# Multiplying ones in TensorE's gaps through the routing stage of a convolution-attention and expert kernel on one core

## The chip, the cores and the metric

One core of a Trainium2 chip runs the whole program. The metric is the device time of one execution in microseconds; the median of the runs is compared.

## What is computed

The input x is 2 images of 256 channels by 32 by 32, so 2048 tokens of 256 channels, float32. First comes a layer norm over channels, then an attention block with 1x1 convolutions (queries, keys and values of 128 channels, a global vector beside the map), whose output is added to x. Then each token is normalised again and routed: a softmax over 8 experts, of which the best two count.

```python
gate = softmax(xt @ Wg); topv, topi = top_k(gate, 2)
topv = topv / (sum(topv) + 1e-6); scores = zeros(T, 8).at[topi].set(topv)
for e in range(8):
    h = gelu(xt @ W1[e] + b1[e])          # 256 -> 1024
    out = out + (h @ W2[e] + b2[e]) * scores[:, e:e+1]
```

The result is added to the tokens.

## The kernel before

The kernel is written by hand for each engine: every engine has its own program, in program order, and engines wait for each other on semaphores that count upwards. Nothing is scheduled by a planner.

It has three stages. In the first (to about 95 us) rows are normalised and projected and the attention runs in 16 row blocks. In the second, which overlaps the end of the first, the tokens are normalised again and routed. In the third the experts run over tiles of gathered tokens. Every product of float32 values is made of three matmuls of split operands (`product3`, L1244 to L1246, and L1545, L1547, L1549 in the second layer).

**Routing.** TensorE turns the normalised tokens (`turn_tokens`, L1414, eight turns of four transposes), ScalarE copies each turn out of PSUM (`xt_copy`, L702), TensorE multiplies with the gate's weights (`logits`, L1429, eight times four float32 matmuls of 8 columns). VectorE takes each half of the tokens in turn: `route_gates` finds the two best experts (L1002 to L1030), TensorE counts ranks within each expert (`ranks`, L1439 and L1440), `route_ranks` (from L1040) turns ranks into places, and VectorE, ScalarE and GpSimd write one-hot matrices (`hot_q` L1066, `hot_r` L501, L733, L1075). TensorE multiplies them (`inverse`, L1455) to get the inverse of the placing, ScalarE copies it (`slot_t`, L773), TensorE makes the table of slots (L1514), and VectorE makes from it the row numbers (`row_in` L1158, `row_out` L1160). VectorE's `route_gates(1)` waits for all eight logits, its `hots(1)` for the first inverse.

**The first gather.** GpSimd waits for `row_in`, raises `gathers_begun`, and gathers three blocks of 128 rows with indirect DMAs (L521). TensorE meanwhile multiplies a matrix of ones into a PSUM bank that nobody reads (10 matmuls, L1573), waits for the gather, turns the rows (`turn_x`, L1522), and multiplies ones 8 times more (L1577). ScalarE and VectorE split the turned rows (`x_hi` L780, `x_lo` L1175), and with that the first tile can start.

**The experts.** Each expert has a first tile, of three blocks (`If(odd)`, L1582) or of two (`Else`), and then a hardware loop over further tiles of two blocks (L1587). A loop over pairs of experts holds this text twice, for the even and for the odd expert, so that TensorE's code for a pair is: three-block tile, two-block tile, loop body, and the same again. A tile of two blocks issues 96 matmuls for the two layers and six transposes, a tile of three blocks 120 and six; each comes with a weight load, so that they are 204 and 252 instructions, and some 15 to 20 waits and register instructions. In an expert's first tile the weights of the next are split by ScalarE (`w_hi` L803) and VectorE (`w_lo` L1202) between the pieces of work for this one, and SyncE loads the ones after that (`load_expert`, L350 and L352).

A float32 matmul of ones stands in the trace as two weight loads and two matmuls: the ten of L1573 are 20 records of each.

Of the kernel before, what the change touches and what calls it, by code (L numbers as in the profile page):

```python
# [24 lines left out]
P = 128  # L25
# [27 lines left out]
def metaformer_kernel(nc, x_tok_d, q1_d, q2_d, k1_d, k2_d, v_d, o_d, aff_d, og_d, ob_d,  # L53
                      wg_d, w1_d, b1_d, w2_d, b2_d, out_d):
    ctx = ExitStack()
    with ctx:
        def sb(name, shape, dt=F32, stack=ctx):
            return stack.enter_context(nc.sbuf_tensor(name, shape, dt))

        def sem(name):  # L60
            return ctx.enter_context(nc.semaphore(name))
# [6 lines left out]
        ones = sb("ones", [P, P])  # L68
# [151 lines left out]
        banks = ctx.enter_context(nc.psum_tensor("banks", [P, 8, 512], F32))  # L220
# [50 lines left out]
        xt_copied = sem("xt_copied")  # L271
# [38 lines left out]
        gathers_begun = sem("gathers_begun")  # L310
# [97 lines left out]
        def _(pool):  # L408
# [162 lines left out]
            for e in range(E):  # L571
                _, t1, odd, more = expert_bounds(pool, e)

                odd1 = pool.value_load(bounds[0:1, 1, e:e + 1], min_val=0, max_val=E)
                with pool.If(odd):
                    tile(t0, e, t0 * 2 + odd0, WIDE)
                with pool.Else():
                    tile(t0, e, t0 * 2 + odd0, 2)
                with pool.If(more):
                    with pool.Fori(t0 + 1, t1) as t:  # L580
                        tile(t, e, t * 2 + odd1, 2)
                t0 = t1
                odd0 = odd1
# [6 lines left out]
        def _(act):  # L590
# [224 lines left out]
            for e in range(E):  # L815
                _, t1, odd, more = experts[e]
                with act.If(odd):
                    tile(t0, e, WIDE, True)
                with act.Else():
                    tile(t0, e, 2, True)  # L820
                with act.If(more):
                    with act.Fori(t0 + 1, t1) as t:
                        tile(t, e, 2, False)
                t0 = t1
# [3 lines left out]
        def _(dve):  # L828
# [397 lines left out]
            for e in range(E):  # L1226
                _, t1, odd, more = experts[e]
                prior = e - 1 if e else None
                with dve.If(odd):
                    tile(t0, e, WIDE, True, prior)  # L1230
                with dve.Else():
                    tile(t0, e, 2, True, prior)
                with dve.If(more):
                    with dve.Fori(t0 + 1, t1) as t:
                        tile(t, e, 2, False, e)
                t0 = t1
# [4 lines left out]
        def _(pe):  # L1241
# [155 lines left out]
            def turn_tokens(i):  # L1397

                if i in (1, 3):
                    pe.wait_ge(xn2_more, i + 1)  # L1400
                else:
                    pe.wait_ge(xn2_ready, {0: 2, 2: 4}.get(i, 2 * i - 2))

                if i in (0, 2):
                    pe.wait_ge(o_taken, i + 2)
                elif i == 3:
                    pe.wait_ge(pt_split, 2 * NBLK)
                elif i in (4, 6):
                    pe.wait_ge(ctx_split, 3 + i // 6)
                else:  # L1410
                    pe.wait_ge(xt_copied, {1: 1, 5: 3, 7: 4}[i])
                for j in range(2):
                    for k in range(KC):
                        ins = pe.transpose(banks[:, XT_BANK[i], (KC * j + k) * P:(KC * j + k + 1) * P],  # L1414
                                           xn2[:, 2 * i + j, k * P:(k + 1) * P], ident[:, :])
                ins.then_inc(xt_ready, 1)

            def logits(n):

                pe.wait_ge(xt_copied, n + 1)  # L1420
                if n == 0:
                    pe.wait_ge(pt_split, 2 * NBLK)
                elif n == 4:
                    pe.wait_ge(o_taken, 7)
                half = n // (HALF // 2)
                for i in (2 * n, 2 * n + 1):
                    c = i % HALF * E
                    for k in range(KC):
                        ins = pe.matmul(banks[:, LG_BANK[half], c:c + E], xt2[:, i, k, :], w_g[:, k, :], start=k == 0,  # L1429
                                        stop=k == KC - 1)  # L1430
                ins.then_inc(lg_ready, 1)

            def ranks(half):

                pe.wait_ge(sel_ready, half + 1)
                chosen = sel[:, :, :].rearrange("p e i -> p (e i)")
                pe.wait_ge(o_taken, 6 + 2 * half)
                bank = banks[:, RANK_BANK[half], :]
                pe.matmul(bank[:, 0:E * HALF], below[:, :], chosen, start=True, stop=True)  # L1439
                pe.matmul(bank[:, E * HALF:2 * E * HALF], ones[:, :], chosen, start=True, stop=True  # L1440
                          ).then_inc(rank_ready, 1)

            def inverse(half, k):

                pe.wait_ge(xt_copied, 5)
                for i in range(HALF):
                    m = HALF * k + i
                    pe.wait_ge(hot_q_ready, 2 * HALF * half + m + 1)
                    if k == 1:
                        pe.wait_ge(hot_r_more, HALF * half + i + 1)  # L1450
                    elif i < POOL_HOTS:
                        pe.wait_ge(hot_r_ready, POOL_HOTS * half + i + 1)
                    else:
                        pe.wait_ge(hot_r_rest, (HALF - POOL_HOTS) * half + i - POOL_HOTS + 1)
                    ins = pe.matmul(banks[:, INV_BANK, 0:P], hot_q[:, k, i, :], hot_r[:, k, i, :],  # L1455
                                    start=half == 0 and m == 0, stop=half == 1 and m == 2 * HALF - 1)
                if k == 1:
                    ins.then_inc(inv_ready, 1)


            pe.wait_ge(proj_out, len(PROJ) - 2)
            for step in range(NBLK + 1):
                if step == 1:
# [30 lines left out]
            turn_tokens(3)  # L1494
            logits(2)
            logits(3)
            turn_tokens(4)
            turn_tokens(5)
            logits(4)
            ranks(0)  # L1500
            logits(5)
            turn_tokens(6)
            turn_tokens(7)
            logits(6)
            logits(7)
            inverse(0, 0)
            ranks(1)
            inverse(0, 1)
            inverse(1, 0)
            inverse(1, 1)  # L1510

            pe.wait_ge(inv_taken, 1)
            pe.wait_ge(place_ready, 1)
# [4 lines left out]
            def turn_x(n):  # L1518
                pe.wait_ge(x_gathered, (n + 1) * (16 * WIDE))
                for i in range(WIDE):  # L1520
                    for k in range(KC):
                        ins = pe.transpose(banks[:, 6 + k, i * P:(i + 1) * P], xg[:, i, k * P:(k + 1) * P],  # L1522
                                           ident[:, :])
                ins.then_inc(xg_turned, 1)
# [43 lines left out]

            pe.sem_inc(l2_done, HJ)
            pe.wait_ge(slots_ready, 2)  # L1570

            for _ in range(10):
                pe.matmul(banks[:, 0, 0:P], ones[:, :], ones[:, :], start=True, stop=True)  # L1573
            pe.wait_ge(bounds_ready, 2)
            turn_x(0)
            for _ in range(8):
                pe.matmul(banks[:, 0, 0:P], ones[:, :], ones[:, :], start=True, stop=True)  # L1577
            with pe.Fori(0, E // 2) as pair:
                for n in range(2):
                    e = pair * 2 + n  # L1580
# [36 lines left out]
```

## Time and profile before

| | us |
|---|---|
| median of 3 runs | 424.38 (423.72 to 425.94) |
| the profiled execution | 422.75 |
| its span | 421.0 |
| TensorE busy (matmul) | 371.4, 88% |
| VectorE busy | 268.9, 64% |
| ScalarE busy | 247.4, 59% |
| GpSimd busy | 183.4, 44% |
| mean granted clock of TensorE | 0.919 of 2.4 GHz |

The profiled execution took 1.75 us more than its span, and 1.63 us less than the median. A line of the page stands for all instructions of one source line; "idle before" is the time in which the engine stood still just ahead of them, with what ended it. PEclk is the share of 2.4 GHz that was granted, so that 0.50 is 1.2 GHz. "issue" is a wait that no semaphore of the profile explains.

### The profile page before, as it was taken

Reading aid. Unit: us, or ns where it says so; the run is one execution under the profiler, and the core shown is the slowest. Engines: PE = TensorE matmul, PEld = TensorE weight load, DVE = VectorE, ACT = ScalarE, POOL = GpSimd, SP = SyncE. Lnnn points to the kernel's source line nnn. Section 1 sums busy time; section 2 is a strip of 40 time slices with the busy share of each in tenths; the row PEclk is TensorE's granted clock in tenths of the full one; section 3 lists DMA queues with packets and bytes.
Section 4 is the critical chain, followed back from the end, with each engine's and each line's share of the span. In section 5 each row is a group of like instructions: output and inputs, shape, how many; then the busy total and the mean of one; then the engine's idle time right before and its main releaser. Section 6 shows DMA issues by size and latency. Waiting matters only on the chain.

```text
span 421.0 us, 8173 instructions
## 1 busy us (share of the span) xinstructions
PE 371.4 (88%) x2476; PEld 333.1 (79%) x2477; DVE 268.9 (64%) x709; ACT 247.4 (59%) x522; POOL 183.4 (44%) x271
## 2 busy tenths in 40 slices
PE   5989978998897958799969999999999999999950
PEld 4535457886786947799969999998999999999950
DVE  5857387798789898275526643975549753945530
ACT  1476656657424774385538654986558864955520
POOL 5800000003035534306664556676667637666553
PEclk8689999999998555899997999999999999999995
DMA  8800000000002655707332653278432913333342
GB/s 267 266 20 2 0 1 2 0 2 1 1 2 100 243 184 205 248 8 251 64 65 29 182 119 53 39 245 229 93 61 29 264 39 54 49 55 59 54 59 29
DMA packets 22966, 38.63 MB, mean 92 GB/s; under 512 B 2576, under 2 KB 17296, under 8 KB 22800
## 3 DMA queue, kind: packets, MB, share of 16 engines
q0 software_dynamic: 8032, 12.82, 17.8%
q1 hardware_dynamic: 14896, 25.41, 17.5%
q8 instruction: 11, 0.18, 0.2%
q14 instruction: 27, 0.22, 0.2%
HBM read 28.85 MB, written 9.37 MB: 91 GB/s over the span
## 4 chain that ended last, share of the span: by engine, by line
PE 36%; issue 8%; POOL 6%; DMA 3%; ACT 3%; DVE 3%; POOLq 1%; DVEq 0%; ACTq 0%
PE banks L1244 6%; PE banks L1245 6%; PE banks L1246 6%; PE banks L1545 5%; PE banks L1547 5%; PE banks L1549 5%; POOL xg L521 4%; DMA xg<-xn_rows,idx_in 3%; PE banks L1522 2%; POOL out_rows L567 2%; ACT h_hi L793 1%; DVE y_out L1184 1%; PE banks L1577 1%; DVE h_lo L1193 1%; DVE w_lo L1202 1%
## 5 line engine op out<-in xcount | busy, mean ns | idle before, releaser
L790 ACT ACTIVATE h_raw<-banks,b1t 128x256 f32<-128x256 f32 (+1 forms) x136 | 68.1, 501 | 79.9 <-PE banks L1246 79.6
L1193 DVE TENSOR_TENSOR h_lo<-h_raw,h_hi 128x256 fp32r<-128x256 f32 (+1 forms) x136 | 58.7, 442 | 71.4 <-ACT h_hi L793 70.6
L567 POOL DMA_INDIRECT out_rows<-y_out,idx_out x36 | 69.5, 1931 | 44.7 <-DVE y_out L1184 38.9
L1545 PE MATMUL banks<-w_hi,h_hi 128*128 128x256 f32 x288 | 83.5, 290 | 1.6 <-DVE h_lo L1193 1.5
L1245 PE MATMUL banks<-x_lo,w_hi 128*128 128x256 f32 (+1 forms) x272 | 79.8, 293 | 3.2 <-issue 3.2
L1244 PE MATMUL banks<-x_hi,w_hi 128*128 128x256 f32 (+1 forms) x272 | 80.6, 296 | 2.2 <-DVE w_lo L1202 1.6
L1549 PE MATMUL banks<-w_hi,h_lo 128*128 128x256 f32 x288 | 81.5, 283 | 0.0
L1547 PE MATMUL banks<-w_lo,h_hi 128*128 128x256 f32 x288 | 81.5, 283 | 0.0
L1246 PE MATMUL banks<-x_hi,w_lo 128*128 128x256 f32 (+1 forms) x272 | 79.7, 293 | 0.0
L521 POOL DMA_INDIRECT xg<-xn_rows,idx_in x57 | 57.8, 1014 | 27.8 <-POOL idx_in L516 16.3
L793 ACT ACTIVATE h_hi<-banks,b1t 128x256 fp32r<-128x256 f32 (+1 forms) x136 | 68.0, 500 | 0.0
L1545 PEld LDWEIGHTS banks<-w_hi,h_hi 128*128 128x128 f32 x288 | 55.2, 192 | 2.6 <-DVE h_lo L1193 2.6
L1244 PEld LDWEIGHTS banks<-x_hi,w_hi 128*128 128x128 f32 x272 | 53.2, 196 | 3.5 <-issue 3.5
L1246 PEld LDWEIGHTS banks<-x_hi,w_lo 128*128 128x128 f32 x272 | 53.3, 196 | 3.3 <-issue 3.3
L1547 PEld LDWEIGHTS banks<-w_lo,h_hi 128*128 128x128 f32 x288 | 55.3, 192 | 0.0
L1549 PEld LDWEIGHTS banks<-w_hi,h_lo 128*128 128x128 f32 x288 | 55.1, 191 | 0.0
L1245 PEld LDWEIGHTS banks<-x_lo,w_hi 128*128 128x128 f32 x272 | 53.2, 196 | 0.0
L472 POOL TENSOR_TENSOR rt<-rstd_i,rhv 128x4 f32<-128x4 f32 x12 | 2.5, 212 | 101.3 <-DVE rstd_i L990 100.6
L1202 DVE TENSOR_TENSOR w_lo<-w_raw,w_hi 128x512 fp32r<-128x512 f32 x56 | 38.5, 688 | 1.2
L803 ACT ACTIVATE w_hi<-w_raw 128x512 fp32r<-128x512 f32 x56 | 37.4, 667 | 0.0
L680 ACT ACTIVATE pt_hi<-banks 128x512 fp32r<-128x512 f32 x32 | 17.5, 596 | 20.9 <-PE banks L1359 20.9
L910 DVE TENSOR_REDUCE rmax<-banks 128x1 f32<-128x1024 f32 x16 | 19.5, 1220 | 7.2 <-PE banks L1246 7.2
(220 smaller groups left out, 673.4 us busy)
## 6 DMA issues: line engine op xcount, KB each, us to landing
w_raw<-in_w SPq DMA_DIRECT2D x16, 1024.0 KB, 8.0
xn_rows<-xn SPq DMA_DIRECT2D x2, 1056.0 KB, 5.2
x<-in_x_tok SPq DMA_DIRECT2D x4, 512.0 KB, 5.3
out_rows<-x SPq DMA_DIRECT2D x1, 2048.0 KB, 9.7
b2b<-in_b SPq DMA_DIRECT2D x1, 1024.0 KB, 4.7
xg<-xn_rows,idx_in POOLq DMA_INDIRECT x57, 3.6
out_rows<-y_out,idx_out POOLq DMA_INDIRECT x36
out_rows<-x POOLq DMA_DIRECT2D x1, 384.0 KB
```

The lines of the kernel that those rows point to most:

```text
L521: pool.indirect_dma_start(xg[:, i, :], None, xs_d, bass.IndirectOffsetOnAxis(ap=idx_in[:, i:i + 1], axis=0)).then_inc(x_gathered, 16)
L567: pool.indirect_dma_start(out_d, bass.IndirectOffsetOnAxis(ap=idx_out[:, i:i + 1], axis=0), y_out[:, i, :], None, compute_op=ALU.add).then ...
L790: act.activation(h_raw[j % RING][:, 0:w], banks[:, j % RING, 0:w], ACT.Gelu, bias=bias)
L793: act.activation(h_hi[:, j, 0:w], banks[:, j % RING, 0:w], ACT.Gelu, bias=bias).then_inc(gelu_done, 1)
L1193: dve.tensor_tensor(h_lo[:, j, 0:w], h_raw[j % RING][:, 0:w], h_hi[:, j, 0:w].bitcast(F32), ALU.subtract).then_inc(h_split, 1)
L1202: dve.tensor_tensor(w_lo[(e + 1) % 2][:, c], w_raw[(e + 1) % 2][:, c], w_hi[(e + 1) % 2][:, c].bitcast(F32), ALU.subtract).then_inc(w_spli ...
L1244: pe.matmul(out, a_hi, b_hi, start=start, stop=False)
L1245: pe.matmul(out, a_hi, b_lo, start=False, stop=False)
L1246: return pe.matmul(out, a_lo, b_hi, start=False, stop=stop)
L1545: pe.matmul(out, h_hi[:, j, r], w_hi[e % 2][:, c], start=j == 0 and i < 2, stop=False, skip_group_check=width == WIDE)
L1547: pe.matmul(out, h_hi[:, j, r], w_lo[e % 2][:, c], start=False, stop=False, skip_group_check=width == WIDE)
L1549: ins = pe.matmul(out, h_lo[:, j, r], w_hi[e % 2][:, c], start=False, stop=j == HJ - 1, skip_group_check=width == WIDE)
```

## The change

A helper `keep_busy(count, bank)` multiplies ones `count` times, into bank 5 unless told otherwise. It is called at eight places of the routing stage (7, 3, 4, 2, 4, 8, 10 and 1 times, 39 in all), with a wait for the eighth copy of turned tokens ahead of `logits(6)`. Behind the table, the 10 matmuls of ones are followed by a wait for `gathers_begun` and by 18 more; behind the first turn of gathered rows there are 5 in place of 8. Nothing else is touched: TensorE's program has 54 more matmuls of ones, all ahead of the loop over experts.

```diff
+            def keep_busy(count, bank=5):
+
+                for _ in range(count):
+                    pe.matmul(banks[:, bank, 0:P], ones[:, :], ones[:, :], start=True, stop=True)
+
...
             logits(2)
             logits(3)
+            keep_busy(7)
             turn_tokens(4)
             turn_tokens(5)
+            keep_busy(3)
             logits(4)
             ranks(0)
             logits(5)
+            keep_busy(4)
             turn_tokens(6)
             turn_tokens(7)
+            pe.wait_ge(xt_copied, 8)
+            keep_busy(2)
             logits(6)
             logits(7)
+            keep_busy(4)
             inverse(0, 0)
+            keep_busy(8)
             ranks(1)
             inverse(0, 1)
+            keep_busy(10)
             inverse(1, 0)
             inverse(1, 1)
+            keep_busy(1)
 
             pe.wait_ge(inv_taken, 1)
             pe.wait_ge(place_ready, 1)
...
             pe.wait_ge(slots_ready, 2)
-
-            for _ in range(10):
-                pe.matmul(banks[:, 0, 0:P], ones[:, :], ones[:, :], start=True, stop=True)
+            keep_busy(10, 0)
+            pe.wait_ge(gathers_begun, 1)
+            keep_busy(18, 0)
             pe.wait_ge(bounds_ready, 2)
             turn_x(0)
-            for _ in range(8):
-                pe.matmul(banks[:, 0, 0:P], ones[:, :], ones[:, :], start=True, stop=True)
+            keep_busy(5, 0)
             with pe.Fori(0, E // 2) as pair:
```

## Rows read from the trace of the kernel before

**Rows 1.** Stages by window: us; busy us (instructions) of PE, PEld, DVE, ACT, POOL; clock; DMA share; GB/s.
```profile
134.00:135.00 1.00, 0.93 (x4) 0.53 (x4) 0.87 (x8) 0.97 (x2) 0.08 (x1) 0.64 0.00 0
...
171.00:172.00 1.00, 1.00 (x11) 1.00 (x10) 0.00 (x0) 0.38 (x1) 0.39 (x2) 0.91 0.83 66
...
175.00:176.00 1.00, 1.00 (x6) 1.00 (x6) 0.00 (x0) 0.00 (x0) 0.84 (x1) 0.88 1.04 369
```

**Rows 2.** Waits of VectorE, 134 to 163 us: waiting line, released by: total us, times, longest.
```profile
DVE incl L1040 <- PE banks L1440: 1.0, 2, 0.8
DVE row_in L1158 <- PE banks L1514: 0.8, 1, 0.8
```

**Rows 3.** TensorE in order of time, 130 to 176 us: start, length, work, [idle before].
```profile
130.25 1.95 PE L1429 MATMUL banks<-w_g,xt 128*128 128x8 f32 x16 [0.25 <-ACT xt L702]
134.04 2.10 PE L1414 MATMUL banks<-ident,xn 128*128 128x128 f32 x8 [1.84 <-ACT xn L697]
136.86 1.87 PE L1429 MATMUL banks<-w_g,xt 128*128 128x8 f32 x8 [0.71 <-ACT xt L702]
...
150.62 0.69 PE L1439 MATMUL banks<-sel,below 128*128 128x64 f32 x2 [2.31 <-DVE sel L1021]
...
163.24 4.64 PE L1573 MATMUL banks<-ones 128*128 128x128 f32 x20 [0.76 <-DVE row_out L1160]
170.74 0.85 PE L1522 MATMUL banks<-ident,xg 128*128 128x128 f32 x6 [2.87 <-DMA xg<-xn_rows,idx_in]
171.42 3.25 PE L1577 MATMUL banks<-ones 128*128 128x128 f32 x16
174.32 0.67 PE L1244 MATMUL banks<-x_hi,w_hi 128*128 128x384 f32 x1
```

**Rows 4.** VectorE in order of time: the picks of half 0, and the split of gathered rows.
```profile
137.68 0.28 DVE L1021 TENSOR_TENSOR sel<-hot_e 128x64 f32<-128x64 f32 x1
...
172.47 0.96 DVE L1175 TENSOR_TENSOR x_lo<-banks,x_hi 128x768 fp32r<-128x768 f32 x1 [3.58 <-ACT x_hi L780]
```

**Rows 5.** TensorE in order of time: an idle stretch of the attention; the second expert's start.
```profile
98.02 1.17 PE L1359 MATMUL banks<-ident,prob 128*128 128x128 f32 x8 [1.51 <-DVE pt_lo L941]
...
217.13 0.38 PE L1244 MATMUL banks<-x_hi,w_hi 128*128 128x256 f32 x1
...
220.74 0.37 PE L1245 MATMUL banks<-x_lo,w_hi 128*128 128x256 f32 x1 [3.23 <-issue]
```

**Rows 6.** TensorE's branches of L1582 at 216 and at 190 us: duration ns, first and last start.
```profile
L1582 PEldq COMPARE_BRANCH  x1: 362/362/362, 216.4 to 216.4; - x1
...
L1582 PEldq COMPARE_BRANCH  x1: 642/642/642, 190.3 to 190.3; - x1
```

**Rows 7.** DMA queues: page, 217 to 221, 40.6 to 138.3, 0 to 170, 170 to 242 us: packets, MB.
```profile
q8 instruction: 11, 0.18, 0.2%
...
q8 instruction: 1, 0.02, 1.5%
...
q8 instruction: 4, 0.07, 0.3%
...
q8 instruction: 5, 0.08, 0.2%
...
q8 instruction: 6, 0.10, 0.6%
```

**Rows 8.** Stages by window, columns as in rows 1.
```profile
40.60:138.30 97.70, 86.91 (x471) 68.35 (x469) 76.62 (x202) 54.74 (x97) 13.58 (x55) 0.98 0.03 12
...
220.70:226.40 5.70, 5.66 (x27) 5.66 (x27) 3.44 (x9) 4.40 (x11) 1.38 (x1) 0.50 0.05 11
226.40:232.10 5.70, 5.70 (x50) 5.70 (x49) 4.27 (x9) 5.07 (x12) 3.42 (x4) 1.00 0.40 47
```

**Rows 9.** SyncE's queue at 191 us; the page's line on such loads (KB each, us to landing).
```profile
191.03 0.37 SPq L350 DMA_DIRECT2D w_raw<-in_w  x1
...
w_raw<-in_w SPq DMA_DIRECT2D x16, 1024.0 KB, 8.0
```

## The prediction

> **What bounds the kernel now.** I read the stages by window first. TensorE's granted clock falls from 2.4 to 1.2 GHz in the microsecond from 134 us; it is up again ahead of 171, falls in the microsecond from there, and rises in the one from 175 (0.88 is a quarter at 1.2 GHz, so at about 175.24) [rows 1]. Each fall follows an idle stretch: 1.84 us ahead of the turns at 134.04, 2.87 us ahead of the first turn of gathered rows [rows 3]. An idle of 1.51 us in the attention brought none [rows 5]. So the change goes at something real. But a slow TensorE costs only where somebody waits for it, which the waits say: from 134 to 163 us VectorE is the engine that sets the time, and it waits for TensorE for 1.0 us at the ranks (0.8 and 0.2) and 0.8 us at the table [rows 2]. From 163 to 174 the path is gather, turn, split, first tile. From 174 on TensorE is nearly always busy and sets the end, so what comes earlier there comes off the time.
>
> The waits of the third stage show one more thing. The first tile of the second expert issues its first matmul at 217.13, the next real start is 220.74, and the 3.23 us between have no semaphore behind them ("issue") [rows 5]. Just ahead stands the branch over the three-block version of the tile, at 216.4 [rows 6], and in that stretch queue q8 moved one packet [rows 7]. The clock then stays at 1.2 GHz to 226.4 [rows 8]. I read this as TensorE waiting for its own program.
>
> **The sum, part by part.** The profiled execution took 422.75 us; the median of the runs is 424.38, 1.63 above. I make the sum against the first and add 1.63.
>
> Price of the ones. 20 records of L1573 take 4.64 us and 16 of L1577, of which the first few are faster, 3.25 [rows 3]: about 0.21 us each without the run-out of the last, so 0.43 us a multiplication at 1.2 GHz, and half, 0.21, at 2.4.
>
> Ranks and table. If the clock stays up, logits(4), 1.87 us for 8 records at 1.2 GHz, takes what logits(2) and (3) took at 2.4, 1.95 for 16, so 0.95 [rows 3], and ends at 137.8 in place of 138.7. `sel` is there at 137.96 [rows 4], so the ranks start 0.7 us earlier and run twice as fast. That covers the wait of 0.8, and the 0.2 at the second ranks. Of the 0.8 at the table ScalarE's copy and the semaphores remain; I take 0.4 off. Together 1.4 us, bounds 0 (clock still falls) and 1.8 (both waits whole).
>
> The 39 ones of the routing stage. Seven behind logits(3) take 1.5 us of an idle stretch of 1.84; three take 0.6 ahead of the 0.71 at logits(4); the 8 ahead of the second ranks take 1.7 of 2.31 [rows 3], which has grown by what logits and inverse gain. The later groups stand where TensorE waits for VectorE's one-hot matrices. The wait for the eighth copy holds back logits(6), but logits(7) had that wait anyway, and VectorE, which shows no wait for it [rows 2], comes to the eighth logits only behind all one-hot matrices of half 0. Cost: nothing, with those gaps as cover. At 1.2 GHz seven would take 3.0 us and push the turns back by 1.2, with ScalarE's copies behind them; I keep that for the range.
>
> The first gather. 28 ones at 2.4 GHz take 6.0 us; the stretch from 163.24 to the landing at 170.7 is 7.5 [rows 3]. `gathers_begun` is raised before the first of the three indirect DMAs, so that wait is over when TensorE comes to it. Cost nothing; idle ahead of the turn falls from 2.87 to about 1.5 us. With the clock at 1.2 throughout they would take 12.0 and hold the turn up by 4.5.
>
> Behind the first turn. `x_lo` ends at 173.43 [rows 4], but the first tile starts at 174.32, because the last of the eight ones were still in front of it [rows 3]. Five at 2.4 GHz end near 172.7. Gain 0.85 us. Then the tile's first matmuls run at 2.4 instead of 1.2 GHz until 175.24: half of 0.92 us, 0.45. Sum of the first part: 1.4 + 0.85 + 0.45 = 2.7 us.
>
> The program itself. This is the part that the change does not speak of: 54 more multiplications of ones, each two weight loads and two matmuls, are 216 more instructions ahead of the expert loop. q8 moved 0.18 MB in 11 packets, 16 KB each [rows 7]; four of them fall in 40.6 to 138.3 us, where TensorE ran straight on with 471 + 469 recorded instructions [rows 7, 8]. That is 235 a packet and, with waits, about 250. So the program comes in blocks of some 250 instructions, and since the stop lies between the first two matmuls of the tile, a block boundary lies there. Behind the branch TensorE had two matmuls to run and then waited for a block asked for at the branch: 216.4 to 220.74, 4.35 us. Shifting the code by 216 moves the boundary 250 - 216, some 35 to 40 instructions, further into the tile: 17 to 20 matmuls at 0.12 us (50 in 5.7 us [rows 8]) are run while the block comes. I take 18 more than now: 2.1 us, and the stop shrinks from 3.2 to 1.1. Idle of 1.1 us is below the 1.51 that left the clock up [rows 5], so the stretch at 1.2 GHz goes as well: its 27 matmuls took 5.7 us and take 3.1 at 2.4 GHz [rows 8], 2.6 less. The splits of ScalarE and VectorE do not get faster with the clock; I give back 0.3 for them. The same shift puts a boundary about 30 instructions behind the other landing, in the loop of the first expert, where now no stop shows. The branch is at 190.3 [rows 6], the block would be there 4.35 us later, at 194.65; TensorE starts that tile at 192.4 and has 14 matmuls, to 194.1. A new stop of 0.5 us. Second part: 2.1 + 2.6 - 0.3 - 0.5 = 3.9. Bounds: nothing, if the boundary is not where I put it, and 5.8 (the old stop and its slow stretch gone).
>
> The Trainium skill (Runtime: NRT & Kernel Launch, Instruction fetch mechanics) says that instructions are refilled in blocks of 16 KiB, 256 instructions, that the next block is fetched while one is executed, and that a taken branch out of that window stops the engine; with exactly 256 the boundary moves by 40 and 20 matmuls are covered, which would make the sum 0.2 us better. By that rule, the trace agrees: the 16 KB packets and the stop behind the branch.
>
> Sum: 422.75 - 2.7 - 3.9 = 416.15, and with 1.63 added 417.8 us, 1.6% below 424.38.
>
> **The rivals.**
> Only the clock part: the stop stays as long as it is (my boundary is off, or the fetch is held up otherwise). For it: one stop in one trace is thin. Against: place, packet and branch fit. 424.38 - 2.7 = 421.7.
> Nothing: the ones do not keep the clock up (idle of 1 to 2.4 us remains ahead of the second ranks), they are only hidden, and the stop stays: 424.4. That is also the case in which the change doesn't do what it says.
> Slower: the new boundary in the first expert's loop. The block for it is asked for at 190.3, and at 191.03 SyncE starts the first of two loads of 1 MB that take 8 us to land [rows 9, 6]. If the packet gets behind them, it comes 8 instead of 4.35 us after the branch: the stop is 4.2 us, and 2.6 more for the clock that then falls. That turns 417.8 into 424.1; it decides from some 2 us more on, 426 to 427, which needs the old stop to stay too or the ones to be late at the turn (4.5 us at most). Another price of the same shift: the loop over pairs now touches seven blocks instead of six. Behind the five q8 packets up to 170 us and the six up to 242, eleven in all [rows 7], none came, so six stay on chip; were seven too many, each of three further passes would stop at least once, 3 x (4.35 + 2.6) = 21 us, 438. The same section of the Trainium skill gives TensorE 128 KiB, eight such blocks, by which this does not happen; no run here shows it yet.
>
> **The numbers.** Forecast 0.58; only the clock part 0.17; nothing 0.11; slower 0.10; better than forecast (no stop at all, 415.5) 0.04. A measurement of this kernel tells about 0.5%, 2.1 us, from no change: faster means below 422.3. Faster: 0.58 + 0.04 + 0.13 of the clock-only case = 0.75; same 0.15; slower 0.10. The range runs from 414.5, the best of the bounds, to 423.5, over the clock-only case; what is left out is the slower cases and most of "nothing".
>
> **What would show it.** Right: PEclk 1.00 from 130 to 176 us, no wait of VectorE for L1440, first tile within 0.2 us of `x_lo`, the "issue" stop of the second expert near 1 us and later within the tile (behind about the twentieth matmul), clock 1.00 behind it, 11 or 12 packets on q8. Wrong: a stop of over 3 us at either landing, clock 0.50 behind it, q8 packets after 245 us, or the turn of gathered rows later than the landing because ones are still running.

## The result, and the profile after

The kernel after takes **420.37 us** (median of 22 runs, 417.68 to 425.96) against 422.75 (22 runs, 420.54 to 426.37) for the kernel before on the same chip: ratio 0.9936, 95% interval 0.9912 to 0.996. That is 0.64%, 2.7 us, where the two medians differ by 2.4: a ratio leaves out runs over 1.5% above the fastest of their kernel (here the one of 425.96 us), a median does not. Forecast was 1.6%. Direction and range held, the size did not: less than half of it came. By its number the result lies nearer to the rival "only the clock part" (421.7, 0.6%) than to the forecast (417.8). The experiments show that it is not that rival: the stop did shrink, and the ones did not bring the gain.

The page of the profiled execution (421.84 us, span 420.1; before 422.75 and 421.0): busy times, tenths of the clock in 40 slices, and the program's queue.

```profile
span 420.1 us, 8389 instructions
PE 376.3 (90%) x2584; PEld 340.0 (81%) x2585; DVE 268.9 (64%) x709; ACT 247.5 (59%) x522; POOL 187.0 (45%) x271
...
PEclk8699999999995995999999999999999999989995
...
q8 instruction: 12, 0.20, 0.2%
```

The packet count is the twelve that the prediction allowed. Next the stages by window, columns as in [rows 1]. The first three answer to [rows 1], the fourth shows the clock from ahead of the first ones on, the last answers to the 1.2 GHz stretch of [rows 8].

```profile
134.00:135.00 1.00, 1.00 (x7) 1.00 (x6) 0.96 (x13) 0.27 (x1) 0.76 (x4) 0.50 0.00 0
171.00:172.00 1.00, 1.00 (x11) 1.00 (x11) 0.00 (x0) 0.00 (x0) 0.00 (x0) 1.00 0.69 127
175.00:176.00 1.00, 1.00 (x8) 1.00 (x7) 0.00 (x0) 0.01 (x1) 0.80 (x1) 1.00 1.09 380
127.50:137.00 9.50, 9.50 (x46) 9.27 (x45) 9.02 (x54) 3.54 (x7) 5.47 (x26) 0.50 0.02 8
220.50:226.20 5.70, 5.70 (x48) 5.70 (x49) 5.48 (x13) 5.70 (x15) 4.17 (x2) 1.00 0.10 20
```

At the second expert the clock holds: 48 matmuls in 5.70 us, where before had 27. In the routing it does not. From 127.5, ahead of the first ones, to 137.0 it is at 1.2 GHz. What that does stands in TensorE's order of time (columns as in [rows 3]):

```profile
132.94 3.33 PE L1464 MATMUL banks<-ones 128*128 128x128 f32 x14
136.06 1.67 PE L1414 MATMUL banks<-ident,xn 128*128 128x128 f32 x8
...
162.92 8.96 PE L1464 MATMUL banks<-ones 128*128 128x128 f32 x56 [0.76 <-DVE row_out L1160]
171.72 0.82 PE L1536 MATMUL banks<-ident,xg 128*128 128x128 f32 x6
172.37 1.28 PE L1464 MATMUL banks<-ones 128*128 128x128 f32 x10
174.65 0.44 PE L1244 MATMUL banks<-x_hi,w_hi 128*128 128x384 f32 x1 [0.99 <-DVE x_lo L1175]
...
219.76 0.28 PE L1245 MATMUL banks<-x_lo,w_hi 128*128 128x256 f32 x1
220.44 0.38 PE L1246 MATMUL banks<-x_hi,w_lo 128*128 128x256 f32 x1 [0.39 <-issue]
...
371.43 0.39 PE L1559 MATMUL banks<-w_hi,h_hi 128*128 128x256 f32 x1 [2.26 <-DVE h_lo L1193]
```

Four things are to be seen. The seven ones behind logits(3) take 3.33 us in an idle stretch of 1.84, and the turns behind them start late. The 28 ones at the gather run straight into the turn, which shows no idle time ahead of it. The stop at the second expert is 0.39 us, behind the twentieth matmul of the tile, where it was 3.23 behind the first [rows 5]. And there is an idle time of 2.26 us at 371, which the first profile of before does not have. VectorE's wait for the ranks shows the first of these from the other side; it was 1.0 in all in [rows 2]:

```profile
DVE incl L1040 <- PE banks L1440: 2.3, 1, 2.3
DVE row_in L1158 <- PE banks L1528: 0.8, 1, 0.8
```

Where the time went, by the start of `x_lo` in each of the 18 tiles, after less before: +0.95 us at the first tile, +0.27 at the fourth (the second expert's first, in which the stop is), -4.77 at the fifth, -4.35 at the fifteenth, -0.91 from the sixteenth on. So this one pair of profiles says: nothing from the ones, 5.0 us from the stop, 3.4 given back at one tile. The experiments show that two of these three numbers are of that pair and not of the change.

One thing helps to read what follows. Each run comes with the mean granted clock. In 12 runs of the unchanged kernel it was 0.922 to 0.931, and those are of two kinds: five runs at 0.922 or 0.923 with a median of 423.51 us, seven at 0.928 to 0.931 with 420.81. The profile that the prediction was made from, at 0.919, is of the slower kind. The 22 runs of the kernel after lie from 0.932 to 0.971, and the time goes with it: 15 runs at 0.95 or more have a median of 418.94 us, the 7 below it 423.2. The profiled one, at 0.948, is of the second kind.

### The profile page after: what moved, and what is told of

Its sections match the earlier page's. It is cut to its first block, busy times and chain, and to the rows that moved or that the text cites. A ratio compares the mean times of both kernels' runs of the same rounds, so it can differ in the third digit from the quotient of the medians.

```text
span 420.1 us, 8389 instructions
## 1 busy us (share of the span) xinstructions
PE 376.3 (90%) x2584; PEld 340.0 (81%) x2585; DVE 268.9 (64%) x709; ACT 247.5 (59%) x522; POOL 187.0 (45%) x271
## 4 chain that ended last, share of the span: by engine, by line
PE 54%; DVE 17%; issue 10%; ACT 7%; POOL 7%; DMA 2%; POOLq 1%; DVEq 0%; ACTq 0%
PE banks L1244 8%; PE banks L1246 7%; PE banks L1245 7%; PE banks L1559 6%; PE banks L1561 5%; PE banks L1563 5%; PE banks L1464 3%; PE banks L1282 3%; POOL out_rows L567 2%; POOL xg L521 2%; PE banks L1359 2%; PE banks L1536 2%; DMA xg<-xn_rows,idx_in 2%; DVE rmax L910 2%; DVE hot_q L1066 2%
## 5 line engine op out<-in xcount | busy, mean ns | idle before, releaser
L1193 DVE TENSOR_TENSOR h_lo<-h_raw,h_hi 128x256 fp32r<-128x256 f32 (+1 forms) x136 | 59.0, 442 | 65.0 <-ACT h_hi L793 53.4
L567 POOL DMA_INDIRECT out_rows<-y_out,idx_out x36 | 73.8, 2049 | 41.8 <-DVE y_out L1184 36.0
L1244 PE MATMUL banks<-x_hi,w_hi 128*128 128x256 f32 (+1 forms) x272 | 79.7, 293 | 2.9 <-DVE w_lo L1202 1.3
L1245 PE MATMUL banks<-x_lo,w_hi 128*128 128x256 f32 (+1 forms) x272 | 78.9, 290 | 0.0
L1244 PEld LDWEIGHTS banks<-x_hi,w_hi 128*128 128x128 f32 x272 | 52.3, 192 | 4.4 <-issue 4.2
L1246 PEld LDWEIGHTS banks<-x_hi,w_lo 128*128 128x128 f32 x272 | 52.3, 192 | 0.6 <-issue 0.6
L1245 PEld LDWEIGHTS banks<-x_lo,w_hi 128*128 128x128 f32 x272 | 52.3, 192 | 0.0
L1202 DVE TENSOR_TENSOR w_lo<-w_raw,w_hi 128x512 fp32r<-128x512 f32 x56 | 38.5, 688 | 1.1
```

What stands on the lines that cost most here:

```text
L567: pool.indirect_dma_start(out_d, bass.IndirectOffsetOnAxis(ap=idx_out[:, i:i + 1], axis=0), y_out[:, i, :], None, compute_op=ALU.add).then ...
L1193: dve.tensor_tensor(h_lo[:, j, 0:w], h_raw[j % RING][:, 0:w], h_hi[:, j, 0:w].bitcast(F32), ALU.subtract).then_inc(h_split, 1)
L1202: dve.tensor_tensor(w_lo[(e + 1) % 2][:, c], w_raw[(e + 1) % 2][:, c], w_hi[(e + 1) % 2][:, c].bitcast(F32), ALU.subtract).then_inc(w_spli ...
L1244: pe.matmul(out, a_hi, b_hi, start=start, stop=False)
L1245: pe.matmul(out, a_hi, b_lo, start=False, stop=False)
L1246: return pe.matmul(out, a_lo, b_hi, start=False, stop=stop)
```

## The experiments

Twelve kernels ran, four to a chip, each against runs of the kernel before on that chip (medians 422.26, 422.43 and 422.06 us).

**First four: which part of the change does it.**

`e1_pad60`, the kernel before with 15 small matmuls near the start, so 60 instructions more and none of the change's ones:

```
+for _ in range(15):
+    pe.matmul(banks[0:16, 7, 0:16], ones[:, 0:16], ones[:, 0:16], start=True, stop=True)
```

> None of the change; 15 matmuls of 16 columns by 16 (60 instructions) stand behind the nine ones at the kernel's start, where TensorE waits anyway from 5 to 7.7 us. They shift TensorE's program by 60 instructions, so that no block boundary lies within 180 instructions behind either landing. If the gain comes from where the block boundary falls: no stop at the second expert (3.2 us), no stretch at 1.2 GHz behind it (2.6 us), 417 us, ratio 0.987 to the kernel before. If the gain comes from the clock in the routing stage: the time of the kernel before, 422.8, ratio 1.000, with the stop still there or moved.

`e2_after_pad40`, the kernel after with 10 of the same, so 256 instructions more than before in all:

```
+for _ in range(10):
+    pe.matmul(banks[0:16, 7, 0:16], ones[:, 0:16], ones[:, 0:16], start=True, stop=True)
```

> The whole change, and 10 small matmuls (40 instructions) at the kernel's start, so that the shift is 256 instructions, one block, and the boundary lies where it lay in the kernel before. If the boundary is the cause: the stop of about 3.2 us between the second and third matmul of the second expert's first tile is back, with the slow clock behind it, 5 us over the changed kernel, ratio to the kernel before 1.00 (0.995 to 1.01). If the clock in the routing stage is the cause: 420.4, ratio 0.994, as the changed kernel.

`e3_routing_only`, the 39 ones of the routing and their wait, 10 and 8 at the gather as before (156 instructions more):

```
-            pe.wait_ge(gathers_begun, 1)
-            keep_busy(18, 0)
...
-            keep_busy(5, 0)
+            keep_busy(8, 0)
```

> Only the 39 ones and the wait of the routing stage; at the gather 10 and 8 as before. The shift is 156 instructions, and no boundary lies near a landing. Boundary theory: 417 to 419.5, ratio 0.986 to 0.992, as the first run, less or more by what the ones bring (at most 1.4 us either way). Clock theory: the ranks' and table's 1.4 us only, 421.4, ratio 0.997.

`e4_gather_only`, 28 ones at the gather and 5 behind the turn, none in the routing (60 instructions more):

```
-            keep_busy(7)
...
-            pe.wait_ge(xt_copied, 8)
-            keep_busy(2)
...
```

> Only the ones at the gather (28 and 5), none in the routing stage. The shift is 60 instructions, the same as in the first run, so that the two differ by those ones alone. Boundary theory: no stop, 417 us, ratio 0.987; against the first run up to 1.3 us less where the clock is at 2.4 GHz at the first tile, and up to 1.5 us more where the 28 ones run at 1.2 GHz and are late at the turn. Clock theory: 421.5, ratio 0.997.

Measured: e1 422.67 us, ratio 0.9986 (0.9958 to 1.0014); e2 421.83, 0.9987 (0.9955 to 1.0019); e3 419.73, 0.9944 (0.9921 to 0.9967); e4 424.06, 1.0026 (0.9987 to 1.0065). Only e3 has a gain, as large as the whole change. e2 has all the ones of the change and its blocks where before has them, and differs from before by nothing that is clear of noise. TensorE's order of time at the second expert, one row of e1, one of e2, one of e4:

```profile
218.95 0.38 PE L1244 MATMUL banks<-x_hi,w_hi 128*128 128x256 f32 x1 [3.12 <-issue]
```

```profile
216.51 0.28 PE L1245 MATMUL banks<-x_lo,w_hi 128*128 128x256 f32 x1 [2.13 <-issue]
```

```profile
216.23 0.38 PE L1244 MATMUL banks<-x_hi,w_hi 128*128 128x256 f32 x1 [0.67 <-issue]
```

With 256 instructions more than before (e2) the stop is back between the tile's first two matmuls, exactly where 0 more had it. With some 235 recorded instructions to a packet of 16 KB [rows 7, 8], a block of the program is thus **256 instructions**, and the place of the stop is that of a block's start. 216 more (after) put it behind the twentieth matmul, 156 more (e3) left no stop at either landing. 60 more (e1) moved it ahead of the tile. There the branch itself took the time, and TensorE stood for 3.12 us (the fence of e1). TensorE's branch in the listing of that line, duration in ns and start:

```profile
L1584 PEldq COMPARE_BRANCH  x1: 3507/3507/3507, 215.0 to 215.0; - x1
```

That is a new price that neither of my theories had: at 60 more, a block starts near the end of the loop that is being left, and in e1 it was fetched only when it was reached. e4 has the same 60 and lost only 0.67 us there: its packet on the program's queue started at 213.4 us, ahead of the branch, and e1's at 216.0, behind it. Why it was asked for sooner stays open.

**Second four: the loss at the sixteenth tile, and blocks against ones.** In after and e1 to e4 alike, 3.4 to 3.8 us of lead over the first profile of before were lost between the fifteenth and sixteenth tile (14 and 15 in the expectations, which count from 0). GpSimd in order of time in the kernel after:

```profile
356.44 5.93 POOL L567 DMA_INDIRECT out_rows<-y_out,idx_out  x1 [1.92 <-DVE y_out L1184]
362.67 1.58 POOL L567 DMA_INDIRECT out_rows<-y_out,idx_out  x1 [0.30 <-issue]
...
366.19 1.04 POOL L521 DMA_INDIRECT xg<-xn_rows,idx_in  x1 [0.87 <-POOL idx_in L516]
...
369.79 0.20 POOL L559 COPY idx_out<-row_out 128x3 uint32 x1
```

One issue of an add took 5.93 us, the next 1.58. The three gathers behind it, and the signal `y_free` behind those, are late by that much; VectorE waits with `y_out` (3.17 us, its longest wait in that stretch), and TensorE for `h_lo`. The experiments move GpSimd's signal ahead of its gathers:

```
 def tile(t, e, block, width):
+    pool.wait_ge(y_added, block * 16 + 16)
+    pool.tensor_copy(idx_out[:, :], ...).then_inc(idx_out_set, 1)
+    pool.wait_ge(idx_out_set, t + 1)
+    pool.sem_inc(y_free, 1)
     pool.wait_ge(scores_moved, t + 1)
...
     gather(t + 2)
-    pool.wait_ge(y_added, block * 16 + 16)
...
```

`e5_before_order` has this alone; `e6_after_order` is the kernel after with it; `e7_pad156_order` the kernel before with it and 39 small matmuls at the start; `e8_routing_order` is e3 with it.

> The kernel before, with one step of GpSimd moved: in each tile the copy of idx_out and the signal y_free stand ahead of the next gather, not behind it. What it is for: in the kernel after, 4.35 us of gain stood at tile 14 and 0.91 us at tile 15; GpSimd issued the adds of tile 13 late (L567 took 5.93 us where it usually takes 1.6), its gather came late behind them, and y_free stood behind the gather, so that VectorE and then TensorE waited. Theory A (y_free behind the gather is what gives the gain back): in the kernel before y_free just comes in time, so this alone changes little: ratio 0.997 to 1.001, tile 15 at its time of before. Rival B (the order of GpSimd has no part in it): the same here, so this run is the base for the other three.

> The kernel after with the same step of GpSimd moved. Theory A: the idle time of TensorE between tiles 14 and 15 (2.26 us in the kernel after) and the fall of its clock behind it (1.7 us) go, the lead at tile 15 stays what it was at tile 14 within 0.7 us, and the time is 2 to 3.5 us below the kernel after: ratio to the kernel before 0.984 to 0.989. Rival B (the adds' descriptors, held back while VectorE runs without a gap, delay the gather itself, and what is late is the gathered tile): TensorE then waits at turn_x for x_gathered instead, the lead is still lost, ratio 0.992 to 0.996.

> The kernel before with 39 matmuls of 16 x 16 near its start (156 instructions, beside work that waits anyway), no ones anywhere that the change has them, and GpSimd's step moved. Its instruction blocks then begin 93 and 106 instructions behind the two places where the other experts' branches land, as in the run with the routing ones alone. Theory A (where a block begins is what the gain at the second expert is made of, and ones only moved it there): no stop at either landing, lead of 3.5 to 5 us at tile 4 and still there at the end, ratio 0.986 to 0.991. Rival C (the ones' effect on the clock ahead of it matters as much): ratio above 0.993, with the routing run below it by over 0.4%.

> The 39 ones of the routing alone, with GpSimd's step moved; blocks begin at the same places as in the run with 39 small matmuls, so the two differ by the routing ones alone. Theory A with ones that give little in the routing: the same time as that run within 0.3%. Rival C (the routing ones keep the clock up and take 1.4 us off, as forecast): 0.3 to 0.5% below it. Rival D (ones that run at 1.2 GHz delay the turns, as at 132.94 in the kernel after): above it by 0.2% or more.

Measured: e5 425.23 us, 1.0069 (1.0043 to 1.0096); e6 421.3, 0.9946 (0.9914 to 0.9978); e7 421.54, 0.9981 (0.9951 to 1.0012); e8 421.01, 0.9975 (0.9941 to 1.0008). The loss at the sixteenth tile is gone in all four (12.9 to 13.3 us between the two tiles, where after has 16.35), but the time is not: at other tiles the gather now waits until the adds have landed, and TensorE waits for it. One such row, of e6 in TensorE's order of time (L1537 is its turn of gathered rows), below one of an "issue" stop in the first expert's loop, of which more below:

```profile
191.20 0.28 PE L1246 MATMUL banks<-x_lo,w_hi 128*128 128x256 f32 x1 [0.48 <-issue]
...
238.91 1.31 PE L1537 MATMUL banks<-ident,xg 128*128 128x128 f32 x5 [2.27 <-DMA xg<-xn_rows,idx_in]
```

So my remedy was a bad one. e5's expectation was wrong (it costs 2.8 us by the medians), e6 missed theory A's 0.984 to 0.989, and e7 its 0.986 to 0.991. Beside each other the four still tell something. e7 has the blocks of e3 and no ones, and is 3.7 us below e5, which has neither. e8 adds the routing's ones and comes 0.5 us lower, and e6, with all the ones and the blocks of after, 0.2 us lower than e7 (0.35% by the ratios); both are inside the intervals. **The place of the blocks is the gain; the ones are hardly to be seen in the median.** What these runs leave open is a part of up to some 0.4%, by the interval of e2, that the ones might have all the same. The kernel before with 216 instructions of padding and nothing else was not run, so the part of the blocks alone rests on two pairs: e2 against after, and e7 against e5.

**Third four: is the loss the change's at all?** `f1_before_again` is the kernel before, unchanged. In the others VectorE scales `y_out` one step later, which leaves GpSimd's order alone:

```
-                    if j == 0 and prior is not None:
+                    if j == 1 and prior is not None:
                         y_scaled(t - 1, prior)
```

`f2_before_late_y` is before with it, `f3_after_late_y` after with it, `f4_routing_late_y` is e3 with it and 5 ones in place of 8 behind the first turn.

> The kernel before, unchanged, for a second profile of it and for what two medians of one kernel differ by. In the first profile of before the tile after tile 14 came without a wait, while the kernel after and all four experiments with GpSimd's order unchanged lost 3.3 to 3.7 us there. Theory A (the change, by coming earlier, makes GpSimd late there): no loss here again, tile 14 to tile 15 takes 12.9 us. Rival E (the loss is there in most executions of before too, and the first profile of it was an exception): 16.3 us from tile 14 to tile 15. Ratio 0.998 to 1.002 by both.

> The kernel before, with VectorE scaling y_out behind the second h_lo of the next tile and not behind the first, so that a late y_free holds up one h_lo less. Theory A: no loss to be had back in before, ratio 0.999 to 1.002. Rival E: the loss at tile 15 is in most executions of before and goes with this, ratio 0.991 to 0.995.

> The kernel after with the same step of VectorE moved. Both theories: TensorE's idle time between tiles 14 and 15 falls from 2.26 us to under 1 us and the clock holds behind it, so 2 to 3.4 us less than the kernel after: ratio 0.985 to 0.989. Against both (the wait moves to a later h_lo or to the next gather): ratio 0.992 to 0.996.

> The ones of the routing with 10 at the gather and 5 behind the first turn, and the same step of VectorE moved; 144 instructions more than before, so that the blocks begin 105 and 118 instructions behind the two landings. If the eighteen more ones at the gather, which are still running when the gather has landed while the clock is at 1.2 GHz, cost time (turn_x at 171.72 in the kernel after, with no idle time ahead of it), this is 0.5 to 1 us below the run of the kernel after with the same step: ratio 0.982 to 0.988. If they are worth what was forecast of them (nothing), the same as that run within 0.2%.

Measured: f1 422.59 us, 1.0013 (0.998 to 1.0047); f2 420.02, 0.9952 (0.9926 to 0.9978); f3 415.5, 0.9887 (0.9835 to 0.9939); f4 **414.9, 0.9834 (0.9791 to 0.9878)**. f3 and f4 ran 6 times each, the others 12. Of f4's six runs four took 414.15 to 415.25 us and two took 422.78 and 425.05; its ratio and interval rest on the four. f1's second profile of the same kernel settles two points. TensorE in order of time, and two windows (columns as in [rows 1]):

```profile
218.08 0.28 PE L1245 MATMUL banks<-x_lo,w_hi 128*128 128x256 f32 x1 [2.40 <-issue]
...
371.77 0.39 PE L1545 MATMUL banks<-w_hi,h_hi 128*128 128x256 f32 x1 [2.18 <-DVE h_lo L1193]
```

```profile
218.10:223.80 5.70, 5.70 (x48) 5.70 (x48) 3.92 (x10) 4.93 (x12) 1.92 (x1) 1.00 0.13 28
371.80:375.00 3.20, 3.20 (x27) 3.20 (x28) 1.35 (x4) 0.89 (x3) 2.46 (x2) 1.00 0.15 16
```

The wait at 371 is in the kernel before too (rival E). Its GpSimd row is the same to the hundredth, 5.93 us. Between the two tiles f1 needs 14.84 us, the first profile of before 12.91, after 16.35 with its clock fallen behind the idle time. And the stop at the second expert is 2.40 us with the clock **at 1.00 behind it**, 48 matmuls in 5.70 us: what I took 2.6 us for was in one profile and not in the other. Three more profiles have a block start at that place. In e2 (stop 2.13 us) the clock holds too. In f2 (2.28) and e5 (2.37) it falls, for half as long as in the first profile of before; the windows, f2's and e5's:

```profile
219.00:222.40 3.40, 3.40 (x18) 3.40 (x18) 1.71 (x4) 2.83 (x7) 0.00 (x0) 0.50 0.21 45
```

```profile
217.30:220.70 3.40, 3.40 (x18) 3.40 (x18) 2.12 (x7) 3.08 (x8) 0.66 (x2) 0.50 0.35 84
```

The stop itself was the longest of the five in the profile that I had. There the packet started at 218.5 us, 2.1 behind the branch; in the other four it started 1.0 to 1.1 us behind it.

f2 gives 2.0 us on the kernel before, and f3 against f2 is 0.9887 / 0.9952 = 0.9935, the same as the change without that step (0.9936), though f3's interval is half a per cent wide either way. As far as that tells, the step and the change add up, and the change gives nothing back there that the kernel before would keep. In f3 the ones' part can be seen when it goes well. Its clock still falls, for most of 126 to 130 and of 143 to 147, but is back when the first seven ones run:

```profile
126.00:130.00 4.00, 4.00 (x22) 3.77 (x22) 3.79 (x18) 0.95 (x2) 2.23 (x11) 0.57 0.24 100
131.30:133.00 1.70, 1.70 (x17) 1.70 (x17) 1.53 (x10) 1.68 (x4) 0.08 (x1) 1.00 0.00 0
143.00:147.00 4.00, 4.00 (x24) 4.00 (x22) 3.93 (x34) 3.90 (x12) 0.42 (x1) 0.57 0.99 394
171.00:176.00 5.00, 4.92 (x30) 4.93 (x31) 2.24 (x4) 3.58 (x8) 1.91 (x3) 1.00 1.02 342
```

```profile
131.28 1.81 PE L1464 MATMUL banks<-ones 128*128 128x128 f32 x14
...
160.25 8.09 PE L1464 MATMUL banks<-ones 128*128 128x128 f32 x56 [0.76 <-DVE row_out L1160]
168.18 0.82 PE L1536 MATMUL banks<-ident,xg 128*128 128x128 f32 x6
```

```profile
DVE row_in L1158 <- PE banks L1528: 0.8, 1, 0.8
```

The first fence is the windows, the second TensorE's order of time, the third VectorE's waits: the one for the ranks is gone, the one for the table is as it was. To compare executions I count from the matmul behind the last 0.62 us wait of out_conv (126.54 in the first profile of before, 125.06 in after, 124.55 in f3), ahead of which nothing of the change stands:

| us from there to | before | f1 | e1 | e4 | after | e2 | f3 | e3 | f4 |
|---|---|---|---|---|---|---|---|---|---|
| VectorE's scan of the ranks | 13.18 | 13.18 | 13.17 | 13.18 | 14.67 | 12.29 | 12.29 | 12.30 | 12.29 |
| table taken (`row_in`) | 35.97 | 35.94 | 35.93 | 35.94 | 37.14 | 35.00 | 34.98 | 38.67 | 34.95 |
| turn of gathered rows | 44.20 | 43.69 | 44.11 | 45.59 | 46.66 | 43.69 | 43.63 | 46.53 | 42.70 |
| first tile | 47.78 | 47.65 | 48.69 | 48.48 | 49.59 | 46.58 | 46.53 | 50.07 | 46.20 |
| `x_lo` of the second tile | 62.90 | 62.43 | 63.48 | 63.23 | 64.30 | 61.29 | 61.25 | 65.22 | 60.92 |

Without the ones the ranks come at 13.2 every time. With them they come 0.9 us sooner, or, where the clock is at 1.2 GHz while ones run, the routing loses instead: 1.5 us at the ranks in after, 2.7 at the table in e3 (there the 4 ones behind logits(7) took 2.06 us and the 8 ahead of the second ranks 3.33). The 28 ones cost at the gather: e4 turns 1.4 to 1.9 us later than f1 and before, and f3, with its table 1.0 us sooner than f1, turns only 0.06 sooner; f4, with 10, keeps all of that 1.0 at the turn, but has its clock at 1.2 GHz behind the longer idle time there (2.77 us), and starts the first tile only 0.33 us ahead of f3.

How much of this is the ones' work can't be read from the table alone. e5 and e7 have none of the change's ones, and GpSimd's moved step comes only in the tiles. Counted the same way, they have the first tile at 46.68 and 47.74 and the second `x_lo` at 61.39 and 62.93. e5's clock is back at 2.4 GHz ahead of its turn and stays there, without any of the change (in f1 it falls again for 3.4 us), and there the first tile comes as early as in e2 and f3 within 0.15 us:

```profile
168.50 1.95 PE L1578 MATMUL banks<-ones 128*128 128x128 f32 x16
170.74 0.44 PE L1245 MATMUL banks<-x_hi,w_hi 128*128 128x384 f32 x1 [0.29 <-DVE x_lo L1176]
```

The intervals of f4 and f3 overlap, so how much of the ten ones' advantage reaches the end is not settled. f4 is the fastest kernel here by its median (414.9, 7.2 us below before), and its interval lies wholly below that of the change alone (0.9912 to 0.996). But two of its six runs took as long as before or longer, and with four runs in the ratio it is **a candidate and not yet a proven better version**.

## Why the prediction was right or wrong

**What bounds it** held: VectorE sets the routing, TensorE the experts, and a stop of the program stood at the second expert (3.23 us, and 2.13 to 2.40 in four more profiles with a block start there).

**The place of the stop** held. I had 18 matmuls more, behind about the twentieth, and it is behind the twentieth. It is 0.39 us there, against a forecast of 1.1: I had counted 4.35 us from the branch to the resumption, which took 3.3 to 3.5 in the other four profiles with the old place and 3.8 in after. The Trainium skill (Runtime: NRT & Kernel Launch, Instruction fetch mechanics) states blocks of 256 instructions, where I used some 250; by that rule the runs agree, e2 above all. The new stop in the first expert's loop (0.5 us) did not come in after and f3, and came once, in e6, which has the same blocks: 0.48 us, behind the thirteenth matmul of that tile. The 2 MB of weights did not hold a packet up, and the seven blocks stayed on the chip: 12 packets in all, where a refetch would have shown more. That rival falls.

**The size of that part** is the step that failed: "its 27 matmuls took 5.7 us and take 3.1 at 2.4 GHz, 2.6 less". Of five profiles with a block start at that place, the clock fell for 6.8 us in the one that I had, for 3.4 us in f2 and e5, and not at all in f1 and e2. From the fourth tile to the fifth:

| us | before | f1 | e2 | f2 | e5 | after | f3 | f4 | e6 |
|---|---|---|---|---|---|---|---|---|---|
| `x_lo` to `x_lo` | 18.24 | 15.71 | 15.50 | 16.23 | 16.35 | 13.21 | 13.27 | 13.20 | 13.21 |

So, each against its like, the part is worth **2.3 to 3.1 us in four pairs in place of the 3.9**, and 5.0 in the one pair that I had. By ratios it is 2.2 us (e2 against after, 0.9987 against 0.9936), and by medians 3.7 (e7 against e5).

**The ones of the routing "cost: nothing"** failed as a rule and held as a case. The text had the other case ("at 1.2 GHz seven would take 3.0 us and push the turns back by 1.2"; they took 3.33, the ranks came 1.5 later), but priced it only in the range. It is the case in 7 of 22 runs if the mean clock tells them apart, and in the profiled one. The premise behind it, that the clock falls behind the idle time at 134 and not before, did not hold: in after it fell at 127, behind 0.62 us of idle time, ahead of the first ones. f2, which has none of the change's ones, shows the same fall, from 126.8 to 130.2.

**Ranks and table**, 1.4 us: 0.9 to 1.0 where the clock is up. The two waits at the ranks (0.8 and 0.2) go, that at the table stays 0.8; the 0.4 taken off it was wrong.

**28 ones at the gather "cost nothing"**: wrong. They run 8.1 to 9.1 us, as the clock is at 1.2 GHz for a part of them, where I had 6.0. The turn comes 0.9 us later for it (f3 against f4) to 1.9 (e4 against f1), less than the 4.5 that I had for a clock at 1.2 throughout.

**Behind the first turn**, 0.85 and 0.45. This can only be read together with the rest: at the second tile's `x_lo`, behind all of the first part, f3 is 1.65 us ahead of the profile of before from which I had summed 2.7, 1.2 ahead of f1, and 0.14 ahead of e5, which has none of the change. after is 1.4 us behind before there. So even where it goes well the first part is 1.65 us of the 2.7, and less against two other executions without the change.

Between the profiled executions of f2 and f3 there are 6.9 us (span 419.5 and 412.6), about what was forecast, but that is luck: f2's is the slowest of its 12 runs and f3's the fastest of its 6. The medians of the two are 4.5 us apart, their ratios 2.7. The change alone has 2.7, since the stop was sized by one profile in which both the stop and the slow clock behind it were the longest of five, and since the ones brought nothing clear of noise: in some runs, a third if the mean clock tells, they delay what they stand ahead of. Without ones the median gain was no smaller (e7 against e5).

The range held in part by its width, and in part by its base: it was set against 424.38, the median of 3 runs, where 22 runs of before give 422.75. Its best end, 414.5, is 1.0 below what the bounds add up to (422.75 - 3.1 - 5.8 + 1.63 = 415.5).

## What to carry to other kernels

Filler work in an idle gap is free only at the clock at which it fits. Price it at 1.2 GHz, since a low clock is the reason for which it is put there, and keep its last piece short of the landing. A change that adds instructions ahead of a loop moves the starts of the program's blocks: look for an "issue" stop behind a branch, count the instructions from the landing to the next start, and compare against a kernel that has the same count without the change. Before a number of one profile goes into a sum (here the slow stretch, then the missing wait at 371), take a second profile of the same kernel, and look where the profiled execution lies among the runs: f2's, the slowest of 12, and f3's, the fastest of 6, are 6.9 us apart here and their medians 4.5.

## What the runs showed that I had not expected

- A block start shortly ahead of the end of a loop is worse than one in the tile: the branch took 3.51 us and TensorE stood for 3.12 in e1, against stops of 2.13 to 2.40 us (once 3.23) between the tile's first two matmuls. It is not so each time: e4, with its block in the same place, lost 0.67.
- GpSimd's issue of one indirect add takes 1.58 us, and 5.93 where VectorE runs splits (L1193, L1202) almost without a gap from 355.5 to 362.5 us. It ends about where VectorE's stretch does, and the issue at this tile took 4.05 to 6.26 us in every profile with GpSimd's old order. That VectorE holds it up fits; no run took VectorE's work away, so it is argued and not shown. The Trainium skill (GPSIMD Engine Reference, Specifications) has GpSimd share its way to SBUF with VectorE and names instructions with two SBUF inputs, as these splits are, as a case of contention; by that rule the trace agrees, with 5.93 against 1.58 us.
- Idle time and the clock: 2.26 us at 371 had the clock fall behind it in after, 2.18 us at the same place in f1 did not, and 0.62 us had it at 127 in after. Behind the stop at the second expert 2.28 and 2.37 us had it (f2, e5), 2.13, 2.40 and even e1's 3.12 did not. One idle stretch doesn't tell what the clock will do, and I made a condition of 1.51 us from one row [rows 5].
